# Two early loads of a fused convolution and FFN kernel move from SyncE's DMA queue to ScalarE's

## What is computed

```
out = conv1d(x, weight, groups=4, 9 taps, padding 4) + (c @ c_weight.T)[:, :, None] + bias     # x: 128 x 32 x 512
gate, up = qlinear(out, w_gate), qlinear(out, w_up)        # 512 -> 1376, rows of x and of w rounded to 8-bit steps
h = silu(gate) * up
result = x + qlinear(h, w_down)                            # 1376 -> 512
```

## Time and profile before

| | |
|---|---|
| median of the runs | 284.26 us |
| profiled execution, its own time | 284.63 us |
| span of the profiled execution | 282.8 us |
| outside the span | 1.83 us |
| PE busy | 272.3 us (96%) |
| DVE busy | 244.1 us (86%) |
| POOL busy | 207.2 us (73%) |
| ACT busy | 196.4 us (69%) |

### The profile page before, as it was taken

One profiled execution on the slowest core, in us unless ns is written; L12 is line 12 of the kernel. 1 busy time (PEld: TensorE's weight loads), 2 busy tenths in 40 slices (PEclk: granted clock), 3 DMA queues, 4 the chain that ended last, 5 costly groups with the idle time before them and its releaser, 6 DMA issues.

```text
span 282.8 us, 5263 instructions
## 1 busy us (share of the span) xinstructions
PE 272.3 (96%) x1821; PEld 152.3 (54%) x1848; DVE 244.1 (86%) x412; ACT 196.4 (69%) x238; POOL 207.2 (73%) x215
## 2 busy tenths in 40 slices
PE   7898899999999999999999999999999999999994
PEld 4787754464455464644444744744444444444443
DVE  0899999999998979889988779879988889888964
ACT  2349999989588866566888836726788886666820
POOL 1579999997959868666788846846778888667731
PEclk9999999999999999999999999999999999999999
DMA  7999934578369998746589995424556764334255
GB/s 251 410 420 418 423 76 105 187 174 213 70 97 261 229 199 236 209 95 200 134 153 355 253 238 154 129 52 125 127 144 162 153 174 107 90 92 123 51 141 185
DMA packets 81577, 52.41 MB, mean 185 GB/s; under 512 B 69648, under 2 KB 70416, under 8 KB 81424
## 3 DMA queue, kind: packets, MB, share of 16 engines
q1 hardware_dynamic: 81264, 51.79, 66.5%
q10 hardware_dynamic: 288, 0.30, 0.4%
HBM read 26.77 MB, written 8.39 MB: 124 GB/s over the span
## 4 chain that ended last, share of the span: by engine, by line
PE 87%; DVE 3%; POOL 3%; DMA 3%; issue 1%; SPq 1%; DVEq 0%
PE bank L1286 52%; PE bank L1310 26%; PE bank L1188 7%; DMA hq_mem<-w_gate_up 3%; POOL hq_mem L496 2%; DVE gu_max L819 1%; DVE y_part L870 1%; POOL h_mem L496 1%; PE bank L1324 1%; PE bank L1205 1%; POOL xq_mem L523 1%; DVE y_mem L857 0%; PE bank L1235 0%; SPq L331 0%; DVE sg_mem L972 0%
## 5 line engine op out<-in xcount | busy, mean ns | idle before, releaser
L1286 PE MATMUL bank<-wgu_t,xq_mem 128*128 128x512 bf16 (+1 forms) x744 | 153.3, 356 | 1.8 <-ACT xq_mem L673 0.5
L532 POOL TENSOR_TENSOR sg_mem<-sg_mem,gu_scale_row 128x512 f32<-128x512 f32 (+1 forms) x96 | 111.0, 1162 | 41.1 <-ACT sg_mem L685 40.9
L1286 PEld LDWEIGHTS bank<-wgu_t,xq_mem 128*128 128x128 bf16 x768 | 73.7, 98 | 73.9 <-DVE h_mem L904 1.6
L685 ACT ACTIVATE sg_mem<-sg_mem,x_scale 128x512 f32<-128x512 f32 (+1 forms) x96 | 62.9, 673 | 33.5 <-DVE sg_mem L891 33.1
L1310 PE MATMUL bank<-wd_t,hq_mem 128*128 128x512 bf16 (+1 forms) x338 | 78.1, 379 | 0.2
L904 DVE SCALAR_TENSOR_TENSOR h_mem<-bank,x_scale,sg_mem 128x512 f32<-128x512 f32 (+1 forms) x96 | 65.6, 691 | 8.5 <-POOL sg_mem L532 7.3
L891 DVE TENSOR_TENSOR sg_mem<-bank,gu_scale_row 128x512 f32<-128x512 f32 (+1 forms) x96 | 59.9, 627 | 11.3 <-PE bank L1286 11.1
L690 ACT ACTIVATE h_mem<-h_mem,h_inv 128x1376 f32<-128x1376 f32 (+1 forms) x32 | 45.3, 1418 | 24.3 <-DVE h_inv L812 24.3
L1310 PEld LDWEIGHTS bank<-wd_t,hq_mem 128*128 128x128 bf16 (+1 forms) x341 | 33.4, 98 | 39.7
L909 DVE TENSOR_REDUCE h_max<-h_mem 128x1 f32<-128x1376 f32 x31 | 48.8, 1576 | 0.0
L698 ACT ACTIVATE hq_mem<-h_mem 128x1376 bf16<-128x1376 f32 (+1 forms) x32 | 42.0, 1315 | 0.2
(11 more groups left out here) (71 smaller groups left out, 173.2 us busy)
## 6 DMA issues: line engine op xcount, KB each, us to landing
xo_mem<-x SPq DMA_DIRECT2D x24, 256.0 KB, 3.1
out<-xo_mem SPq DMA_DIRECT2D x24, 256.0 KB, 2.2
slab<-x_pairs SPq DMA_DIRECT2D x8, 576.0 KB, 7.7
slab_taps<-x_pairs SPq DMA_DIRECT2D x7, 576.0 KB, 5.7
hq_mem<-w_gate_up SPq DMA_DIRECT2D x7, 512.0 KB, 11.5
slab_taps<-w_down SPq DMA_DIRECT2D x3, 688.0 KB, 14.7
h_mem<-w_gate_up SPq DMA_DIRECT2D x4, 512.0 KB, 16.6
slab_taps<-x SPq DMA_DIRECT2D x1, 2048.0 KB, 9.8
```

Of the source, the lines that this page charges most:

```text
L532: pool.tensor_tensor(s, s, gu_scale_row[:, 1, at:at + n], ALU.mult).then_inc(silu_scaled, 1)
L685: act.activation(s, s, ACT.Silu, scale=x_scale_of(i)).then_inc(silu_done, 1)
L1286: last = pe.matmul(bank[n % 2][:, 0:cols], xq_t[:, g, k, P * c:P * (c + 1)], wgu_t[:, m, k, at:at + cols], start=(k == 0), stop=(k == KT - 1))
```

## The change

The loads of pair 2 and of the other bands are issued by ScalarE, behind its two loads of before, and no longer by SyncE. Sizes, semaphores, sources and destinations stay the same, and no engine's computing instructions change.

```diff
-            def load_other_taps():
-                sp.dma_start(band_rest[:, :], taps).then_inc(taps_rest_in, 16)
...
             load_first()
             load_third()
             load_pair(1)
-            load_pair(2)
-            load_other_taps()
             load_w(0)
             load_w(1)
             load_pair(3)
...
             act.dma_start(small_sb[:, :], cond_ctx_bias).then_inc(small_in, 16)
+            act.dma_start(pair_blocks(2).rearrange("p b n -> p (b n)"), x_pairs[2, :, :]).then_inc(pair_in[2], 16)
+            act.dma_start(band_rest[:, :], taps).then_inc(taps_rest_in, 16)
             act.wait_ge(warm_ready, 1)
             act.activation(silu_trial[:, :], warm_in[:, 0:1], ACT.Silu)
```

## The result

The changed kernel takes 285.3 us (median of 22 executions, 284.77 to 289.76) against 284.9 us before (22 executions beside it, 284.05 to 286.64). The ratio is 1.0036, with a 95% interval of 1.0018 to 1.0053: slower by 0.4%, some 1.0 us. The sign of the forecast holds in the first; its size of 1.5 us is only just reached by the upper end. In the second the interval takes in no change. The ratio of the first is larger than the medians show (0.4 us), because the changed kernel has a long upper tail: 7 of its 22 executions have a mean granted clock of 0.994 or less and take 286.6 to 289.8 us, the other 15 have a median of 285.16. The ratio goes by the fast executions alone, so the two slowest of the changed kernel, 289.62 and 289.76, are not in it.

The account below looks back on a forecast made before the run. The prediction took two paths meeting at the fold at 14.60, weight block 1 and pair 1, to bound the front. Pair 1's 1.6 us delay less 0.05 slack, some 1.5, on 284.26 gave 285.8 us, range 284.4 to 286.6.

Parts of the forecast that it names:

- What bounds the front: Weight block 1 and pair 1's path through ScalarE and GpSimd meet at the fold at 14.60; later delay there reaches the end.
- the side branch of GpSimd: GpSimd's rounding of weight blocks 0 and 1 ends at 18.8, not 17.2, but is in time again by 21.2; costs nothing.
- ScalarE's two issues: 0.9 us of issuing ahead of ScalarE's first copy, hidden in 6.57 us of idle time with over 5 us to spare.
- Pair 1 shares with pair 2: Both queues served about equally, so pairs 1 and 2 land together; pair 1 1.6 us later, bounds 1.4 and 1.9.
- the round by packets: DMA engines go round queues packet by packet; by that alone pair 1 lands at about 8.85 and the sum is 0.15 us smaller.
- The landing at 9.0: Pair 1's load lands at 9.0 us instead of about 7.4, 1.6 us later.
- weight block 1 at 11.8: Weight block 1 still lands at 11.8 us, since the same bytes must be moved before it.
- The bound of 8.85: Earliest landing of pair 1 under equal sharing: 8.85 us, when pair 2 landed before the change.
- The slack of 0.05 us ahead of the fold: Pair 1's path to the fold at 14.60 has 0.05 us of slack to the weight block path, subtracted from 1.6 us.
- The clock: Rival: TensorE's gap before pair 1, about 2.1 us, drops its clock to 1.2 GHz; 288 us or more; chance 0.06.
- The total: Median of 284.26 us before plus 1.5 us gives 285.8 us; range 284.4 to 286.6.
- Unequal shares: Rival: SyncE's queue gets two bytes to ScalarE's one, pair 1 lands at 8.1; delay 0.7 us, 285.0 us; chance 0.18.
- The filled dips: Rival: two queues fill dips in the DMA rate, weight block 1 lands 0.3 us earlier; 284.0 us; chance 0.04.

Follow-up runs that it names:

- pair2_waits: The changed kernel, but ScalarE waits for the small operands before it issues pair 2 and the other bands; 289.68 us, ratio 1.0162.
- after_again: The changed kernel run once more, unaltered, as the second comparison with the kernel before; 285.14 us against 284.89, ratio 1.0004 (0.9984 to 1.0024).
- The filled kernels: The changed kernel, and pair 2 alone moved (two runs), each with nine more empty matmuls on TensorE; ratios to before 1.0032, 1.0027 and 1.0010.
- before_again: The kernel before run once more, unaltered, for a second trace; a single execution, 285.36 us.
- only_pair2_b: The kernel before with only pair 2 issued by ScalarE, run again on another chip; median 285.38 us, ratio 1.0019 (0.9985 to 1.0053).

## Why the prediction was right, and where its steps were off

**What bounds the front: right.** The fold of spans 4 and 5 sets the span, with pair 1's path through ScalarE and GpSimd ahead of it. That is the column of 268.2 to 268.4 us over traces whose folds lie between 14.08 and 16.48. Two smaller points were right too: the side branch of GpSimd costs nothing, and ScalarE's two issues are hidden.

**Pair 1 shares with pair 2: right in kind, a little large in size.** The middle engine's count goes from 6.2 us to 7.3 and 7.5, so by 1.1 to 1.3, against a forecast of 1.4 to 1.9 with 1.4 from the round by packets. The two pairs landed 0.3 us apart, as forecast. The Trainium skill, "DMA: Bandwidth & Descriptors", section "Queues, rings and completion order", says packets are taken in turns from the queues; the 50.3% and 49.4% of 9 to 10 us in pair2_waits agree, and so do the 71 and 72 packets of 12 to 13 us.

**The landing at 9.0 and weight block 1 at 11.8: neither number holds for all executions.** Traces of the changed kernel have pair 1 at 9.8 and 7.9. Weight block 1 lands at 12.9 in the first and at 11.0 in after_again. The bound of 8.85 came from one trace of before, in which pair 1 was the latest of three (7.4, 6.9, 6.6). A landing is set by the slowest of 16 engines, as I read the counts, and this was taken for a number that repeats.

**The slack of 0.05 us ahead of the fold: the term that was mis-sized.** The prediction let the 1.6 us of pair 1 go through but for 0.05, since TensorE waits 0.53 us for pair 1. In two of three traces of before there is no such wait: TensorE's clock rises late, pair 0 takes 3.4 to 3.6 us, and pair 1 has 1.3 to 1.5 us of slack. In such executions a landing at 7.9 should cost nothing. The times fit this. Of the 45 executions of before that ran beside the changed kernel, 12 are under 284.6 us, of its own 34 none. The best starts are lost, the others seem to stay as they were. Over the executions at a clock above 0.994 the medians are 284.89 (all 65 of before) and 285.14: a cost of 0.25 us where 1.5 was forecast, and none where both ran side by side (284.89 and 284.87 beside after_again). The filled kernels, 0.3 to 0.7 us above before by their medians, put the cost higher; some 0.1 us of that is the fill.

**The clock: the place was wrong, and the chance of 0.06 too low.** It falls in 10 of 34 executions, and where a trace shows it, not in the gap before pair 1 but from 25 us on, after stretches in which TensorE waits for the late VectorE. The late chain is the same 2.35 us; what was overlooked is that a delay on VectorE makes TensorE wait some 6 us later (1.13 us ahead of 23.51). The price in the trace is 269.7 less 268.3, or 1.4 us, where the rival had 2 us or more. It is mostly this that brings the mean up to 286.1 from 285.0 and the ratio to 1.0036: the ten have a mean of 288.4 us, the other 24 of 285.2.

**The total: in the range partly by luck.** The 285.8 us stand on a median of three executions of before, 284.26; 22 of them have 284.9. From there the sum gives 286.4, 1.1 us above the measured 285.3, and the low base hid half of that. What was measured, 0.4 us by the medians and 1.0 by the ratio, is made of a delay smaller than forecast and of falls of the clock that the prediction priced at 288 us and gave 0.06.

**The rivals.** Unequal shares are refuted by the 0.44 and 0.42 MB of the two queues in the changed kernel. The filled dips are seen in one trace: at 6 to 7 us the stretches of before_again show 309 GB/s, those of after_again 427; but in the changed kernel's first trace it is 368 at 6 to 7 and 313 at 7 to 8, so this is not a steady gain.

## What to carry to other kernels

Moving a load to an idle issuing engine is also a change of priority: it now shares, packet for packet, with whatever the first queue holds, and if that is the load needed first, it lands later while the total stays the same. Take two or three traces before calling a landing or a slack a number, since the last of a load's 16 counts strays by up to 2.4 us, and TensorE's first microseconds depend on when its clock rises. And follow a delay to the engine that idles because of it much later: here a third of the executions ended with a fallen clock, some 3 us slower in the mean than the others.

## What the runs showed of the hardware that was not expected

- A load issued on an idle queue at 4.89 us, while the other queue was deeply filled, moved no packet until after 8 us; ScalarE's first load, issued at 0.73, moved its first at 2.0. Issued at 1.67, behind the first loads of both queues, pair 2 had about half of the bytes from 4.5 us on. Why is not known.
- The 16 counts of one load can come 3.9 us apart (pair 1 of the changed kernel, 5.9 to 9.8 us), and 0.4 us apart in another execution of a kernel with pair 2 moved (only_pair2_b, 7.4 to 7.8).
- TensorE's clock came to 2.4 GHz at 3.9 us in one execution of the kernel before and at 7.2 us in another, after the same seven empty matmuls. In pair2_waits it fell once right behind a gap of 2.31 us (0.50 in the stretch of 13 to 16 us, below); in the changed kernel it did not after 2.69 us of idle time at 7 to 9.8 us.

```profile
12.00:13.00 1.00, 0.50 (x6) 0.51 (x8) 1.00 (x3) 0.00 (x0) 1.00 (x2) 0.86 1.02 410
13.00:16.00 3.00, 3.00 (x32) 3.00 (x32) 1.44 (x3) 0.00 (x0) 0.01 (x1) 0.50 1.06 428
```
